# Attention masks copied into PSUM by ScalarE instead of added by a matmul on TensorE

## The chip, the cores and the metric

The kernel runs on one core of one Trainium2 chip, as one launch. The metric is the device time of that launch in microseconds (us). The names of the engines are those of the profile: PE is TensorE, PEld its weight loads, DVE is VectorE, ACT is ScalarE, POOL is GpSimd, and SP issues most of the transfers.

## The reference, cut to what matters

Two transformer-like layers on 4 batches of 512 tokens of width 128. The change touches only the attention of layer 0, causal, with 16 heads of width 8:

```
mask  = where(triu(ones(S, S), k=1), -inf, 0)
score = einsum('bhqd,bhkd->bhqk', Q, K) / sqrt(8)
score = score + mask
score = score - max(score, axis=-1)
score = exp(score);  score = score / sum(score, axis=-1)
out   = einsum('bhqk,bhkd->bhqd', score, V)   # then @ WO
```

After it come a mixture of 8 experts, a gated linear recurrence with a feed-forward part, and a network with ternary weights. They stay as they are.

## The kernel before, in words

Attention works in 16 **groups**: 4 batches times 4 sets of 4 heads (`NW = 16`; `b` is the batch, `g` the set). The scores of a group are computed twice.

**Row scores** serve only for the maximum of each row. They are cut into 10 **units** (the table `UNITS`): unit u is a pair (t, k), 128 queries of tile t against the 128 keys of tile k for 4 heads, so one matmul that fills a whole PSUM bank of 128x512 (`row_scores`, L1802 to L1817, the matmul is L1812). In the four diagonal units, t == k, a second matmul (L1815) multiplies an identity with `mask4`, a 128x512 tile with -1e30 above the diagonal, and adds it to the same bank. Before the change the diagonal units are numbers 1, 4, 5 and 9. DVE reduces each bank to its row maxima (`row_max`, L1172) and gives it back by `row_free`. There are three such banks, taken in turn (`RING`, `ROWB = 3`): the matmul of a unit waits until the unit three before it is reduced. When all ten are reduced, DVE makes the negated maxima (`minus_max`, L1178 to L1182), PE turns them (`turn_max`, L1854) and DVE adds them to the queries (`add_max`, L1186).

**Key scores** are the scores that count, with keys on the partitions, in 12 units n = 0 to 11 (`key_scores`, L1828). ACT takes the exponential of each (`exp_unit`, L761), 128x512 for n = 0 to 3 and 128x384 for the rest; three banks as well, so key unit n waits for exponential n-3. POOL zeroes what lies above the diagonal in their output (L634). PE multiplies with the values (`values`, L1840), ACT copies the result out (`store_sums`, L768), PE turns it (`turn_out`, L1862) and DVE normalises it (L1194, L1195).

Every engine's order is written by hand, and each engine works through its own queue in that order. The loop runs over **turns** w = 0 to 15. Turn w on PE holds, among others: row unit 0 of group w+1, `turn_max(w)`, then key units 8 to 11 of group w-1 and 0 to 3 of group w mixed with row units 1 to 8 of group w+1, then `values` 1 to 3 of group w-1, row unit 9, key units 4 and 5, `turn_out(w-1)`, `values(w, 0)`, key units 6 and 7.

From the second batch on, the rest of the previous batch's layer 0 is woven in: in turns 4, 8 and 12 PE turns the heads (L1868) and ACT copies them (`take_turn`, L779), in turns 5, 9 and 13 PE multiplies with WO (`times_wo`, L1874), DVE adds and takes statistics, ACT normalises (`tail_norm`, L797), in turns 6, 10 and 14 PE turns the normed rows (L1882), ACT copies them (L779 again) and PE computes the router's logits (L1888), and in turns 7 and 11 DVE ranks them. In turns 0, 4 and 8 the queries and keys of the next batch are projected too (L1799, L1800, ACT's L751, DVE's L1162).

In the text "row unit 9" is unit 9 of the row scores, "exp 7" the exponential of key unit 7.

Of the kernel before, what the change touches and what calls it, by code (L numbers as in the profile page):

```python
# [6 lines left out]
ACT = mybir.ActivationFunctionType  # L7
# [13 lines left out]
NG = 4  # L21
# [16 lines left out]
KEYB = 3  # L38
UNITS = [(1, 0), (1, 1), (2, 0), (2, 1), (0, 0), (2, 2), (3, 0), (3, 1), (3, 2), (3, 3)]
PTW = 10 * P  # L40
# [31 lines left out]
def _turns():  # L72

    at = {}
    for w in range(NW):
        before, g = w // NG - 1, w % NG
        at["max", w] = len(at)
        if before >= 0 and g:
            at[("wo", "turn2", "ranks")[g - 1], before] = len(at)
        if before >= 0 and g == 2:  # L80
            at["logits", before] = len(at)
        if w:
            at["out", w - 1] = len(at)
        if before >= 0 and g == 0:
            at["turn", before] = len(at)
    return at
RING = _ring()
TURNS = _turns()
EARLY = {1: 4, 2: 2, 3: 2}

# [25 lines left out]
def build(nc, d):  # L116
    ctx = ExitStack()
    with ctx:
# [220 lines left out]
        pv_done, v_ready = sem("pv_done"), sem("v_ready")  # L339
        mx_done, qm_done = sem("mx_done"), sem("qm_done")  # L340
        varA, rsA, xnA = sem("varA"), sem("rsA"), sem("xnA")
# [382 lines left out]
        def _(act):  # L724
# [28 lines left out]
            def exp_unit(w, n):  # L753
# [4 lines left out]
                if i == 0 and w:  # L758
                    act.wait_ge(pv_done, TB * (w - 1) + js[-1] + 1)
                act.wait_ge(ts_full, NKU * w + n + 1)  # L760
                act.activation(PT[:, i, a:z], bank[ROWB + n % KEYB][:, 0:z - a], ACT.Exp,  # L761
                               scale=float(DK) ** -0.5).then_inc(exp_done, 1)
            def store_sums(w):

# [64 lines left out]
            for w in range(NW):  # L829
# [14 lines left out]
                exp_unit(w, 2)  # L844
                exp_unit(w, 3)
                if w:
                    store_sums(w - 1)
# [8 lines left out]
                if b and g == 1:  # L856
                    tail_numbers(b - 1)
                    tail_norm(b - 1, 0)
                    tail_norm(b - 1, 1)
                exp_unit(w, 6)  # L860
                exp_unit(w, 7)
            exp_unit(NW - 1, 8)
# [902 lines left out]
        def _(pe):  # L1765
# [36 lines left out]
            def row_scores(G, u):  # L1802
# [5 lines left out]
                elif u == 0:  # L1808
                    pe.wait_ge(qs_in[G % 2], 16 * ((G + 1) // 2))
                    pe.wait_ge(kp_in[G % 3], 64 * ((G + 2) // 3))  # L1810
                t, k = UNITS[u]
                mm = pe.matmul(to, QS[:, G % 2, t * P:(t + 1) * P],  # L1812
                               KP[:, G % 3, k, :, :].rearrange("p i n -> p (i n)"), start=True, stop=t != k)
                if t == k:
                    mm = pe.matmul(to, identr[:, :], mask4[:, :, :].rearrange("p i n -> p (i n)"),  # L1815
# [637 lines left out]
```

## Time and profile before

| | us |
|---|---|
| median of 3 runs | 619.7 (617.17 to 621.14) |
| profiled execution, its own time | 618.03 |
| its span in the trace | 616.3 |
| stage the change lies in (turns 0 to 14) | from 26 to 188 |
| PE busy | 576.6 (94%) |
| DVE busy | 413.6 (67%) |
| ACT busy | 329.6 (53%) |
| mask matmuls (L1815) in the trace | 64 |

A row of the timeline gives the start of a run of like instructions, how long it lasts, engine, line, what is written and read, how many, and in brackets how long the engine had been idle and for whom it waited. A matmul of 512 columns lasts some 0.39 us or more from start to end, but the next one starts before it has ended, so matmuls are costed by the distance of their starts and not by their length. The granted clock is 1.00 in the whole stage.

### The profile page before, as it was taken

Reading aid. Unit: us, or ns where it says so; the run is one execution under the profiler, and the core shown is the slowest. Engines: PE = TensorE matmul, PEld = TensorE weight load, DVE = VectorE, ACT = ScalarE, POOL = GpSimd, SP = SyncE. Lnnn points to the kernel's source line nnn. Section 1 sums busy time; section 2 is a strip of 40 time slices with the busy share of each in tenths; the row PEclk is TensorE's granted clock in tenths of the full one; section 3 lists DMA queues with packets and bytes.
Section 4 is the critical chain, followed back from the end, with each engine's and each line's share of the span. In section 5 each row is a group of like instructions: output and inputs, shape, how many; then the busy total and the mean of one; then the engine's idle time right before and its main releaser. Section 6 shows DMA issues by size and latency. Waiting matters only on the chain.

```text
span 616.3 us, 9661 instructions
## 1 busy us (share of the span) xinstructions
PE 576.6 (94%) x3486; PEld 448.1 (73%) x3486; DVE 413.6 (67%) x1012; ACT 329.6 (53%) x582; POOL 177.2 (29%) x196
## 2 busy tenths in 40 slices
PE   7899999999998699999896988999999999998997
PEld 3667676676764479999765776887878877896776
DVE  6788799899884645645679859945688376752420
ACT  5766675675666235766154438525565257533541
POOL 6223132452643735556421240014101130001100
PEclk9999999999999989999998979999999999999999
DMA  4475641442200647751401000000000000000000
GB/s 140 160 278 196 250 135 45 145 127 74 77 27 2 189 136 256 240 203 56 130 1 35 2 0 0 1 1 2 18 1 1 1 1 17 1 2 0 18 0 18
DMA packets 32543, 45.96 MB, mean 75 GB/s; under 512 B 4336, under 2 KB 18160, under 8 KB 32240
## 3 DMA queue, kind: packets, MB, share of 16 engines
q1 hardware_dynamic: 29904, 40.30, 19.9%
q0 software_dynamic: 2304, 4.74, 2.2%
q8 instruction: 28, 0.46, 0.3%
q10 hardware_dynamic: 288, 0.31, 0.1%
q14 instruction: 19, 0.16, 0.1%
HBM read 26.09 MB, written 19.24 MB: 74 GB/s over the span
## 4 chain that ended last, share of the span: by engine, by line
PE 72%; DVE 13%; ACT 7%; issue 5%; POOL 2%; DMA 1%; DVEq 0%; ACTq 0%; POOLq 0%; SPq 0%
PE ps L2204 7%; PE ps L1812 6%; PE ps L1828 5%; PE ps L2226 5%; PE ps L2119 5%; PE ps L1840 5%; PE ps L2227 4%; PE ps L2307 4%; PE ps L2303 4%; PE ps L2304 4%; PE ps L2230 4%; DVE pm L1172 3%; PE ps L2220 2%; PE ps L1815 2%; PE ps L2104 2%
## 5 line engine op out<-in xcount | busy, mean ns | idle before, releaser
L1172 DVE TENSOR_REDUCE pm<-ps 128x4 f32<-128x512 f32 x160 | 102.7, 684 | 16.8 <-PE ps L1812 9.4
L761 ACT ACTIVATE PT<-ps 128x384 f32<-128x384 f32 (+1 forms) x192 | 92.1, 527 | 31.5 <-PE ps L1828 29.0
L634 POOL TENSOR_SCALAR_AFFINE_SELECT PT<-PT 128x512 f32<-128x512 f32 x64 | 40.1, 639 | 115.6 <-ACT PT L761 115.5
L1812 PE MATMUL ps<-KP,QS 128*128 128x512 f32 x160 | 67.6, 437 | 1.8 <-ACT VR L741 0.7
L1828 PE MATMUL ps<-QM,KP 128*128 128x512 f32 (+3 forms) x256 | 65.1, 328 | 0.4 <-ACT PT L761 0.4
L1828 PEld LDWEIGHTS ps<-QM,KP 128*128 128x128 f32 x256 | 42.9, 189 | 18.2 <-ACT PT L761 10.2
L671 POOL DMA_INDIRECT ytok_dram<-zero,rowS x40 | 41.2, 1030 | 34.9 <-DVE zero L1479 24.4
L608 POOL TENSOR_TENSOR rstd<-veps,mhalf 128x4 f32<-128x4 f32 x11 | 12.7, 1154 | 112.6 <-DVE veps L1083 111.2
L1608 DVE TENSOR_TENSOR_SCAN zero<-decay,OG 128x512 f32<-128x512 f32 x32 | 42.0, 1314 | 1.1
L1840 PE MATMUL ps<-PT,V 128*32 128x128 f32 (+3 forms) x512 | 41.5, 439 | 0.0
L973 ACT ACTIVATE hF<-ps,cols 128x512 f32<-128x512 f32 x16 | 11.0, 688 | 55.9 <-PE ps L2307 55.9
L912 ACT ACTIVATE HT<-ps,cols 128x640 f32<-128x640 f32 x32 | 25.5, 796 | 26.0 <-PE ps L2106 25.3
L1812 PEld LDWEIGHTS ps<-KP,QS 128*128 128x128 f32 x160 | 29.9, 188 | 12.7 <-DVE pm L1172 4.8
L1603 DVE SCALAR_TENSOR_TENSOR OG<-ps,cols,vs 128x512 f32<-128x512 f32 x32 | 23.9, 748 | 17.9 <-ACT vs L952 10.3
L2119 PE MATMUL ps<-W,HT 128*128 128x128 f32 x296 | 35.6, 275 | 0.0
L956 ACT ACTIVATE gs<-ps,half_bg 128x512 f32<-128x512 f32 x32 | 22.0, 689 | 24.1 <-PE ps L2230 23.3
L2119 PEld LDWEIGHTS ps<-W,HT 128*128 128x128 f32 x296 | 34.8, 192 | 0.0
L952 ACT ACTIVATE vs<-ps,cols 128x512 f32<-128x512 f32 x32 | 22.0, 687 | 19.4 <-PE ps L2230 19.3
L2204 PEld LDWEIGHTS ps<-lwo,oT 128*128 128x128 f32 x256 | 29.1, 192 | 0.2
L2204 PE MATMUL ps<-lwo,oT 128*128 128x128 f32 x256 | 29.2, 275 | 0.0
L698 POOL TENSOR_TENSOR aT<-OT,aT 128x512 fp32r<-128x512 f32 x12 | 16.9, 1411 | 38.4 <-ACT OT L936 37.0
L680 POOL TENSOR_TENSOR rstd<-veps,mhalf 128x8 f32<-128x8 f32 x3 | 5.3, 1765 | 77.6 <-DVE veps L1569 77.6
(345 smaller groups left out, 1413.5 us busy)
## 6 DMA issues: line engine op xcount, KB each, us to landing
qk_dram<-HL SPq DMA_DIRECT2D x8, 512.0 KB, 3.8
W<-in_eW SPq DMA_DIRECT2D x16, 256.0 KB, 4.8
QS<-qk_dram SPq DMA_DIRECT2D x15, 256.0 KB, 2.7
KP<-qk_dram SPq DMA_DIRECT2D x60, 64.0 KB
xs_dram<-zero SPq DMA_DIRECT2D x4, 645.0 KB, 3.8
XS<-xs_dram SPq DMA_DIRECT2D x8, 322.5 KB, 3.0
qk_dram<-HL SPq DMA_DIRECT2D x8, 256.0 KB, 4.0
ytok_dram<-zero SPq DMA_DIRECT2D x4, 512.0 KB, 4.6
```

What stands on the lines that cost most here:

```text
L634: g.affine_select(out=diag, in_=diag, pattern=[[0, 4], [1, P]], compare_op=ALU.is_ge, fill=0.0, base=0, channel_multiplier=-1).then_inc(se ...
L671: g.indirect_dma_start(out=ytok_dram, out_offset=bass.IndirectOffsetOnAxis(ap=rowS[:, x, j:j + 1], axis=0), in_=YS[:, s, j, :], in_offset= ...
L761: act.activation(PT[:, i, a:z], bank[ROWB + n % KEYB][:, 0:z - a], ACT.Exp, scale=float(DK) ** -0.5).then_inc(exp_done, 1)
L912: act.activation(HT[:, s, f, :].rearrange("p (a n) -> p a n", a=2), ps[:, 2 * (f % 2):2 * (f % 2) + 2, 0:HALF], ACT.Gelu, bias=cols[:, at: ...
L1172: v.tensor_reduce(pm[:, t, k, :], bank[n % ROWB].rearrange("p (i n) -> p i n", n=P), AXX, ALU.max).then_inc(row_free[n % ROWB], 1)
L1608: v.tensor_tensor_scan(st, decay[:, f:f + 1].to_broadcast([P, SEQ]), kv, 0.0, ALU.mult, ALU.add).then_inc(st_done, 1)
L1812: mm = pe.matmul(to, QS[:, G % 2, t * P:(t + 1) * P], KP[:, G % 3, k, :, :].rearrange("p i n -> p (i n)"), start=True, stop=t != k)
L1828: mm = pe.matmul(bank[ROWB + n % KEYB][:, at:at + SEQ - j * P], KP[:, w % 3, j, i, :], QM[:, w % 2, j * P:SEQ], start=True, stop=True)
L1840: mm = pe.matmul(bank[6][32 * i:32 * i + 32, j * P:SEQ], V[:, j * H + g * 4 + i, :], PT[:, i, OFF[j]:OFF[j + 1]], start=(j == 0), stop=(j ...
L2119: mm = pe.matmul(place(j), HT[:, s, f, j * P:(j + 1) * P], W2[:, s, f, :], start=(f == 0 and (j in (PARTS[0][0], PARTS[1][0]) or not follo ...
L2204: mm = pe.matmul(bank[5][:, t * P:(t + 1) * P], src[:, f, t * P:(t + 1) * P], w[:, f, :], start=(f == 0 and t == 0), stop=(f == n - 1), sk ...
L2226: pe.matmul(to, high[n][:, cs], halves_of[:, 0, :], start=True, stop=False)
```

## The change

`UNITS` is put in another order, so that the diagonal units are now numbers 0, 1, 2 and 9. For 50 of the 64 diagonal units, listed in `SEEDS`, ACT copies `mask4` from SBUF into the bank before the scores (`seed`), and the score matmul is issued with start=False, so that it adds to what lies there; it waits for the semaphore `seeded`. The mask matmul of these units is gone. Not listed are all units of groups 0 and 1, and units 1 and 2 of groups 2, 6 and 10; these 14 diagonal units keep the mask matmul. The copy waits, like the score matmul, until the bank's previous unit is reduced. In ACT's queue the copy for unit 9 of group w+1 stands after exp 3 of turn w, those for units 0 and 1 of group w+2 before exp 6 and that for unit 2 between exp 6 and exp 7.

```diff
-UNITS = [(1, 0), (1, 1), (2, 0), (2, 1), (0, 0), (2, 2), (3, 0), (3, 1), (3, 2), (3, 3)]
+UNITS = [(0, 0), (1, 1), (2, 2), (1, 0), (2, 0), (2, 1), (3, 0), (3, 1), (3, 2), (3, 3)]
...
+def _seeds():
+    at = {}
+    for w in range(NW):
+        if 2 <= w + 1 < NW:
+            at[9, w + 1] = len(at)
+        if w + 2 < NW:
+            for u in range(1 if (w + 2) % NG == 2 and w + 2 < NW - 2 else 3):
+                at[u, w + 2] = len(at)
+    return at
...
+            def seed(u, G):
+                if (u, G) in SEEDS:
+                    n = RING[u, G]
+                    act.wait_ge(row_free[n % ROWB], n // ROWB)
+                    act.activation(bank[n % ROWB], mask4[:, :, :].rearrange("p i n -> p (i n)").bitcast(F32),
+                                   ACT.Copy).then_inc(seeded, 1)
...
                 exp_unit(w, 3)
+                seed(9, w + 1)
                 if w:
                     store_sums(w - 1)
...
+                seed(0, w + 2)
+                seed(1, w + 2)
                 exp_unit(w, 6)
+                seed(2, w + 2)
                 exp_unit(w, 7)
...
                 t, k = UNITS[u]
+                sown = (u, G) in SEEDS
+                if sown:
+                    pe.wait_ge(seeded, SEEDS[u, G] + 1)
                 mm = pe.matmul(to, QS[:, G % 2, t * P:(t + 1) * P],
-                               KP[:, G % 3, k, :, :].rearrange("p i n -> p (i n)"), start=True, stop=t != k)
-                if t == k:
+                               KP[:, G % 3, k, :, :].rearrange("p i n -> p (i n)"), start=not sown, stop=t != k or sown,
+                               skip_group_check=sown)
+                if t == k and not sown:
                     mm = pe.matmul(to, identr[:, :], mask4[:, :, :].rearrange("p i n -> p (i n)"),
                                    start=False, stop=True)
```

The first place is ACT's queue in turn 4 and the start of turn 5 (turn 8 reads the same), before the change. HL is the rounded queries or keys of the next batch, OT the turned heads.

```order
63 L751 ACTIVATE HL<-ps 128x512 [waits rs_full,k_planes,q_planes]
64 L751 ACTIVATE HL<-ps 128x512 [waits rs_full]
65 L779 ACTIVATE OT<-ps 128x512 [waits tp_full]
66 L761 ACTIVATE PT<-ps 128x384 [waits ts_full] x2
67 L761 ACTIVATE PT<-ps 128x384 [waits ts_full,pv_done]
```

The same place after the change; L772 is now the exponential, L779 the copy of the mask and L798 `take_turn`.

```order
83 L762 ACTIVATE HL<-ps 128x512 [waits rs_full,k_planes,q_planes]
84 L762 ACTIVATE HL<-ps 128x512 [waits rs_full]
85 L798 ACTIVATE OT<-ps 128x512 [waits tp_full]
86 L779 ACTIVATE ps<-mask 128x512 [waits row_free0]
87 L772 ACTIVATE PT<-ps 128x384 [waits ts_full] x2
88 L772 ACTIVATE PT<-ps 128x384 [waits ts_full,pv_done]
```

The copy for row unit 0 of group 6 has come in behind the copy of the turned heads and ahead of exp 6 and 7.

The second place is PE's queue at the start of turn 5, before the change: row unit 0 of group 6, the turn of the maxima, and what follows up to row unit 3.

```order
226 L1828 MATMUL ps<-QM,KP 128x384 [waits exp_done] x2
227 L1812 MATMUL ps<-KP,QS 128x512 [waits kp_in0,qs_in0,row_free0]
228 L1854 MATMUL ps<-const,MX 128x128 [waits mx_done,tp_free]
232 L1812 MATMUL ps<-KP,QS 128x512 [waits row_free1]
233 L1815 MATMUL ps<-mask,identr 128x512
238 L1812 MATMUL ps<-KP,QS 128x512 [waits row_free2]
239 L1828 MATMUL ps<-QM,KP 128x256 [waits exp_done]
```

The same place after the change (key scores are now L1855, row scores L1838, the mask matmul L1842, the turn of the maxima L1881).

```order
212 L1855 MATMUL ps<-QM,KP 128x384 [waits exp_done] x2
213 L1838 MATMUL ps<-KP,QS 128x512 [waits kp_in0,seeded,qs_in0,row_free0]
214 L1881 MATMUL ps<-const,MX 128x128 [waits mx_done,tp_free]
218 L1838 MATMUL ps<-KP,QS 128x512 [waits row_free1]
219 L1842 MATMUL ps<-mask,identr 128x512
224 L1838 MATMUL ps<-KP,QS 128x512 [waits row_free2]
225 L1842 MATMUL ps<-mask,identr 128x512
226 L1855 MATMUL ps<-QM,KP 128x256 [waits exp_done]
```

Row unit 0 now waits for `seeded` and stands ahead of the turn of the maxima, and row unit 2 of this group has a mask matmul that it did not have.

The third place is PE's queue late in turn 2, before the change, from row unit 9 to the turn of the sums.

```order
129 L1840 MATMUL ps<-PT,V 32x384 [waits sel_done]
133 L1840 MATMUL ps<-PT,V 32x128 [waits sel_done]
135 L1812 MATMUL ps<-KP,QS 128x512 [waits row_free1]
136 L1815 MATMUL ps<-mask,identr 128x512
137 L1828 MATMUL ps<-QM,KP 128x384 [waits exp_done] x2
138 L1862 MATMUL ps<-const,OG 128x128 [waits og_done,tp_free]
140 L1840 MATMUL ps<-PT,V 32x512 [waits og_done,v_ready,sel_done]
```

And after the change (`values` is L1867, the turn of the sums L1889).

```order
124 L1867 MATMUL ps<-PT,V 32x384 [waits sel_done]
128 L1867 MATMUL ps<-PT,V 32x128 [waits sel_done]
130 L1838 MATMUL ps<-KP,QS 128x512 [waits seeded,row_free1]
131 L1855 MATMUL ps<-QM,KP 128x384 [waits exp_done] x2
132 L1889 MATMUL ps<-const,OG 128x128 [waits og_done,tp_free]
134 L1867 MATMUL ps<-PT,V 32x512 [waits og_done,v_ready,sel_done]
```

The mask matmul between row unit 9 and key unit 4 is gone; the turn of the sums still waits for ACT's copy of them (`og_done`).

## Rows read from the trace of the kernel before

**Rows 1.** The page, part 1: busy time, share of the span, instructions

```profile
PE 576.6 (94%) x3486; PEld 448.1 (73%) x3486; DVE 413.6 (67%) x1012; ACT 329.6 (53%) x582; POOL 177.2 (29%) x196
```

**Rows 2.** The page, part 4: the chain that ended last, by engine

```profile
PE 72%; DVE 13%; ACT 7%; issue 5%; POOL 2%; DMA 1%; DVEq 0%; ACTq 0%; POOLq 0%; SPq 0%
```

**Rows 3.** Busy time by window: a plain turn, then turn 7; length, then each engine's

```profile
55.60:65.20 9.60, 9.60 (x72) 6.56 (x71) 7.94 (x16) 6.37 (x14) 2.50 (x4) 1.00 0.48 154
99.10:108.80 9.70, 9.62 (x82) 6.50 (x83) 9.30 (x25) 5.96 (x13) 2.50 (x4) 1.00 0.19 56
```

**Rows 4.** Timeline of DVE in a plain turn, 54 to 65.5 us

```profile
55.68 0.69 DVE L1172 TENSOR_REDUCE pm<-ps 128x4 f32<-128x512 f32 x1 [0.58 <-PE ps L1812]
...
56.88 4.95 DVE L1172 TENSOR_REDUCE pm<-ps 128x4 f32<-128x512 f32 x8
62.72 0.69 DVE L1172 TENSOR_REDUCE pm<-ps 128x4 f32<-128x512 f32 x1 [0.89 <-PE ps L1815]
...
65.29 0.69 DVE L1172 TENSOR_REDUCE pm<-ps 128x4 f32<-128x512 f32 x1 [0.58 <-PE ps L1812]
```

**Rows 5.** Timeline of PE's matmuls in the same turn

```profile
60.53 1.50 PE L1840 MATMUL ps<-PT,V 128*32 128x384 f32 x24
61.96 0.50 PE L1812 MATMUL ps<-KP,QS 128*128 128x512 f32 x1
62.30 0.39 PE L1815 MATMUL ps<-mask,identr 128*128 128x512 f32 x1
62.52 0.52 PE L1828 MATMUL ps<-QM,KP 128*128 128x384 f32 x2
...
64.86 0.40 PE L1812 MATMUL ps<-KP,QS 128*128 128x512 f32 x1
```

**Rows 6.** Timeline of PE's weight loads in the same turn

```profile
60.09 0.19 PEld L1812 LDWEIGHTS ps<-KP,QS 128*128 128x128 f32 x1 [0.30 <-DVE pm L1172]
...
62.81 0.43 PEld L1862 LDWEIGHTS ps<-const,OG 128*128 128x128 f32 x4
```

**Rows 7.** Timeline of ACT in the same turn

```profile
56.36 4.31 ACT L761 ACTIVATE PT<-ps 128x384 f32<-128x384 f32 x8 [0.21 <-PE ps L1828]
62.10 0.60 ACT L768 ACTIVATE OG<-ps 128x512 f32<-128x512 f32 x1 [1.43 <-PE ps L1840]
62.95 0.87 ACT L761 ACTIVATE PT<-ps 128x384 f32<-128x384 f32 x2 [0.26 <-PE ps L1828]
64.88 0.87 ACT L761 ACTIVATE PT<-ps 128x384 f32<-128x384 f32 x2 [1.05 <-PE ps L1828]
```

**Rows 8.** Groups of ACT's instructions by form, 30 to 184 us: busy, mean ns, idle

```profile
L773 ACT ACTIVATE V<-VR 128x512 f32<-128x512 f32 x3 | 1.9, 623 | 0.0
```

**Rows 9.** Timeline of ACT, end of turn 8

```profile
121.04 0.60 ACT L779 ACTIVATE OT<-ps 128x512 f32<-128x512 f32 x1 [0.98 <-PE ps L1868]
121.54 0.87 ACT L761 ACTIVATE PT<-ps 128x384 f32<-128x384 f32 x2
```

**Rows 10.** Timeline of all engines at the start of turn 9

```profile
121.20 0.39 PE L1812 MATMUL ps<-KP,QS 128*128 128x512 f32 x1
...
121.70 0.66 PE L1854 MATMUL ps<-const,MX 128*128 128x128 f32 x4
...
125.37 0.69 DVE L1208 TENSOR_TENSOR X<-ps,X 128x512 f32<-128x512 f32 x1 [0.30 <-PE ps L1874]
```

**Rows 11.** Timeline of ACT, end of turn 5 and turn 6

```profile
86.45 0.88 ACT L797 ACTIVATE xn_rows<-X,nmr,rstd 128x128 f32<-128x128 f32 x2
87.52 0.87 ACT L761 ACTIVATE PT<-ps 128x384 f32<-128x384 f32 x2 [0.20 <-PE ps L1828]
88.78 0.49 ACT L761 ACTIVATE PT<-ps 128x384 f32<-128x384 f32 x1 [0.39 <-PE ps L1828]
...
91.53 0.62 ACT L779 ACTIVATE xn2T<-ps 128x512 f32<-128x512 f32 x1
```

**Rows 12.** Timeline of PE, turn 6

```profile
92.64 0.95 PE L1888 MATMUL ps<-wr,xn2T 128*128 128x8 f32 x8
```

More of the change, by code:

```diff
@@ L86, in _turns @@
     return at
+def _seeds():
[7 more added lines that the diff above has]
+    return at
 RING = _ring()
+SEEDS = _seeds()
 TURNS = _turns()
@@ L339, in build @@
         pv_done, v_ready = sem("pv_done"), sem("v_ready")
-        mx_done, qm_done = sem("mx_done"), sem("qm_done")
+        mx_done, seeded = sem("mx_done"), sem("seeded")
         varA, rsA, xnA = sem("varA"), sem("rsA"), sem("xnA")
```

## The prediction, made before the changed kernel was run

> **What bounds the kernel now.** I read the share of busy time first: PE is busy 94% of the span, ACT and DVE far less [rows 1], and the chain of waits puts 72% on PE [rows 2]. That speaks for taking work off PE. But a busy share adds up matmuls that overlap, and the change lies in one stage, so I went to the windows of that stage. In a plain turn of 9.6 us DVE is busy 7.94, ACT 6.37; in turn 7 DVE is busy 9.30 of 9.70 [rows 3]. So DVE is close behind PE in a plain turn and is the bound in turn 7, as in turn 11, which has the same work.
>
> What a plain turn really waits for shows when the timelines of the engines are laid side by side. DVE reduces row unit 0 at 55.68, then adds the maxima, and from 56.88 reduces units 1 to 8 without a break, 4.95 us for eight, a step of (4.95 - 0.69)/7 = 0.61 [rows 4]. Unit 5 is thus done at 56.88 + 4 x 0.61 + 0.69, near 60.0, and exactly then PE, which sat 0.30 for DVE, loads the weights of row unit 8 [rows 6], the unit that takes the bank of unit 5. Behind it come the values at 60.53 and row unit 9 at 61.96 [rows 5]. ACT, idle 1.43, starts to copy the sums when the values are done, at 62.10, and ends at 62.70 [rows 7]; 0.11 later PE loads the first weights of the turn of the sums, 62.81 [rows 6]. The values of unit 0, key units 6 and 7 and row unit 0 follow, at 64.86 [rows 5], and DVE, idle 0.58 for it, takes that at 65.29 [rows 4]: one turn of 9.61. The loop of the turn is: DVE from unit 0 to unit 5, row unit 8, values, ACT's copy, the turn of the sums, values, key units, row unit 0. **No mask matmul lies on it.** Those of units 1, 4 and 5 lie where PE ends up waiting for DVE; that of unit 9 lies beside ACT's copy of the sums.
>
> **What the change removes.** A mask matmul costs PE the distance to the next start: 62.30 to 62.52, say 0.23 [rows 5]. 50 of them are 11.5 us of PE. In plain turns (1 to 3, 8 and 12) I take the gain as 0.03 each: without the mask PE would be ready for the turn of the sums 0.23 earlier, but ACT's copy ends at 62.70 and the load starts at 62.81 anyway. In turns 7 and 11 DVE is the bound and nothing is gained. Together -0.2.
>
> **What it adds.** 50 copies of 128x512 by ACT. No row shows ACT writing PSUM from SBUF. The nearest are PSUM to SBUF, 0.60 [rows 7], and SBUF to SBUF, 623 ns [rows 8]; I take 0.60 from start to end. When ACT is never idle the next instruction starts 0.50 after such a copy: the turned heads go out at 121.04 and exp 6 starts at 121.54 [rows 9]. So a copy takes 0.50 of ACT's queue. As ends of the range I take 0.50 and 0.75 for the whole length: the step of a queue and half as much again over it. The Trainium skill, "ScalarE: Activation LUTs", section "Step-by-step: what each stage is for", holds that "ScE→PSUM is faster than ScE→SBUF"; no row here shows such a write, and by that rule the lower end, 0.50, would hold and the sum below come out 0.6 lower.
>
> Plain turns: the copy for unit 9 follows exp 3, which ends at 56.36 + 4.31 = 60.67, in an idle stretch of 1.43 [rows 7]. It waits for the reduction of unit 6, near 60.6. Done near 61.3, it is there before row unit 9 at 61.96 [rows 5]. The copies for units 0 and 1 come behind exp 5, which ends at 62.95 + 0.87 = 63.82, in an idle stretch of 1.05 [rows 7]: 2 x 0.50 just fits, and unit 0's is done at 64.4, before row unit 0 at 64.86. The copy for unit 2 pushes exp 7 back by 0.50, and key unit 10 waits for exp 7. There PE loses what the missing mask of unit 1 gave, and DVE, which sets the pace, notices nothing. ACT has 9.6 - 6.4 = 3.2 us free in such a turn [rows 3] and is asked for 2.0. Cost 0, covered by ACT's idle time; should exp 4 to 7 run later than now, it is up to 0.5 per turn (the third rival).
>
> Turns 0 and 1 work on groups 1 and 2, with a mask matmul now on unit 0 (ahead of the turn of the maxima) and on unit 2, where there was none. Each was placed where PE is just in time for DVE: +0.23 each, **+0.5**. The bounds are 0 and 0.9, four masks.
>
> **Turns 5, 9 and 13** hold most of the cost. Now PE issues row unit 0 at 121.20, while ACT copies the turned heads from 121.04, and the turn of the maxima, which waits for that copy to end at 121.64, starts at 121.70 [rows 9, 10]. After the change ACT can begin the mask copy only at 121.54; it ends at 122.14, and row unit 0, which stands ahead of the turn of the maxima in PE's queue, starts near 122.28. The turn of the maxima follows at 122.5 instead of 121.70: +0.8. Between it and the product with WO PE's queue is full, and DVE, idle 0.30 for PE, adds that product at 125.37 [rows 10]; in turns 5 and 9 a mask on unit 2 comes on top, +0.23. In turn 13 a mask less gives 0.23 back, but two more copies ahead of exp 7 make key unit 10 wait some 0.4. So +1.0 three times, **+3.0**; with the ends of the copy's price 2.7 and 3.5.
>
> **Turns 6, 10 and 14.** At the end of the turn before, ACT has no idle time to give: the norms run from 86.45 to 87.33 and exp 6 starts at 87.52 [rows 11]. Three copies there take 1.5 us against idle stretches of 0.20 and 0.39 (before 88.78, where exp 8 starts) and a gap of some 0.1: exp 8 and all behind it come 0.8 later, 0.6 in the other two turns. The copy of the normed rows moves from 91.53 [rows 11] to about 92.4 and ends at 93.1, so that the router's product starts at 93.2 and not at 92.64 [rows 12]; the missing masks between can't help, since it is ACT that is late. +0.5 and twice +0.4, **+1.3**, with bounds 0 and 2.4 (0.8 each). The statistics ahead of it run on DVE and hide nothing.
>
> **Sum:** -0.2 + 0.5 + 3.0 + 1.3 = +4.6 us. What lies behind attention waits for its last group, so I pass this on one to one. The profiled execution took 618.03 us in a span of 616.3; it would take 622.6. It was 1.7 below the median of the runs, 619.7, so for a median I say **624**.
>
> **The rivals.**
> First, PE is the bound, as the shares say [rows 1, 2]. Then 50 x 0.23 = 11.5 us go and the stage gives 608. It decides if DVE could start earlier with what PE brings earlier; against it stand the eight reductions without a break [rows 4] and the 0.30 that PE waits for them [rows 6]. 7%. By the Trainium skill, "TensorE: Matmul & The Clock Gate", section "Back-to-back issue gap", a sustained stream with 512 columns costs 131 ns per matmul, by which this rival would gain only 50 x 0.131 = 6.6 us; the 0.22 between the starts in rows 5 does not agree, and I go by that.
> Second, a part of it: the plain turns gain the mask of unit 9 after all (0.23 x 9 = 2.1), and turns 5, 9, 13 lose half as much as I say: 617 to 619. 8%.
> Third, the copies are hidden everywhere but in a few places: each wait at the start of turns 5, 9 and 13 is swallowed by DVE's own work later in the turn. 618 to 622, that is no change. 20%.
> Fourth, on the slower side beyond my forecast: ACT becomes the bound. The 11 copies for unit 2 push exp 7 back, and in every turn key unit 10 and all behind it come 0.5 late: 11 x 0.5 = 5.5 on top of 4.6, 630. It decides once ACT's late exponentials outlast the 1.43 that it is idle before the copy of the sums [rows 7]. Against it: 0.92 of that are left. 12%.
> The forecast, a loss of 2.5 to 8 us, has the remaining 53%.
>
> A difference of under 1%, 6.2 us, is no change by what a measurement of this kernel can tell. Faster by more is the first rival alone, 7%. Slower by more, over 625.9, is the fourth, 12%, and of the forecast the upper part, about 15%: 27%. The rest is 66%. The range of 8 in 10 takes in the hidden case and the upper bounds of the terms: 617.5 to 629.5.
>
> **What would show it in the changed profile.** L1842 (mask) 14 times, the copy from the mask 50 times at about 0.6. A plain turn of 9.6, with DVE's eight reductions still without a break, and the load for the turn of the sums still 0.11 behind ACT's copy. At the start of turns 5, 9 and 13 row unit 0 waiting for ACT, and the turn of the maxima 0.8 later than ACT's copy of the heads asks for. The router's product 0.4 to 0.5 later in its turn. I am wrong if a plain turn gets shorter than 9.4 or longer than 9.8, or if DVE shows breaks among the eight.

## The result and the profile after

The changed kernel takes 622.2 us (median of 20 runs, 619.6 to 623.5) against 619.7 for the kernel before on the same chip. The ratio is 1.0040 with a 95% interval of 1.0028 to 1.0053: a loss of 2.5 us that can be told from nothing and lies within the 1% that the forecast called no change. The profiled execution has a span of 618.0 us (before 616.3). The page's shares of busy time after the change, beside [rows 1]:

```profile
PE 572.4 (93%) x3436; PEld 436.5 (71%) x3436; DVE 410.3 (66%) x1012; ACT 352.8 (57%) x632; POOL 176.8 (29%) x196
```

PE has lost its 50 matmuls and ACT has gained 50 instructions; where the time went must be read turn by turn. A turn is measured from one reduction `mx<-pm` of DVE (L1178 before, L1201 after) to the next. The last of them, the end of turn 14, in the timeline of DVE before and after:

```profile
186.74 0.26 DVE L1178 TENSOR_REDUCE mx<-pm 128x16 f32<-128x64 f32 x1
```

```profile
189.01 0.26 DVE L1201 TENSOR_REDUCE mx<-pm 128x16 f32<-128x64 f32 x1
```

The attention stage ends 2.27 us later, which is about the loss of the medians. The two profiled spans differ by less, 1.7 us, because what lies behind the stage took 0.6 less in the second. That part isn't equally long from one execution to the next: the kernel before took 429.6 us for it here and 431.4 in a second profile (experiments, third set). So the turns, and not the spans, carry the argument. Lengths of the turns in us, worked out from these rows:

```
turns           0     1   2..4(mean)  5     6     7     8     9    10    11    12    13    14
before       8.19 11.09   9.62   13.39 11.31 10.48  9.42 13.88 11.30 10.42  9.44 12.15 11.31
after        8.41 11.24   9.52   14.47 11.50 10.02  9.15 14.47 11.56  9.95  9.15 13.04 11.96
difference  +0.22 +0.15  -0.10   +1.08 +0.19 -0.46 -0.27 +0.59 +0.26 -0.47 -0.29 +0.89 +0.65
```

**The copy.** The view of line L779 (instructions, their shortest, median and longest duration in ns; then what ended ACT's idle time before them, and who waited for them, in us and times):

```profile
L779 ACT ACTIVATE ps<-mask x50: 577/601/611, 35.4 to 185.1; 128x512 f32<-128x512 f32 x50
...
  DVE pm L1195: 3.7, 11
...
  PE ps L1838: 3.9, 5
```

It takes 0.60 us, as the forecast took it. PE waited for it 3.9 us in 5 places. The Trainium skill's sentence that ScalarE writes PSUM faster than SBUF ("ScalarE: Activation LUTs", section "Step-by-step: what each stage is for") holds here by some 0.02 us, 601 ns against the 623 ns of [rows 8], not by the 0.10 that I gave as its end of the range.

**A plain turn.** DVE in turn 3 (start, busy time, idle before and its releaser), to be laid beside [rows 4]:

```profile
55.98 0.69 DVE L1195 TENSOR_REDUCE pm<-ps 128x4 f32<-128x512 f32 x1 [0.58 <-PE ps L1838]
...
57.18 4.88 DVE L1195 TENSOR_REDUCE pm<-ps 128x4 f32<-128x512 f32 x8
62.71 0.69 DVE L1195 TENSOR_REDUCE pm<-ps 128x4 f32<-128x512 f32 x1 [0.65 <-PE ps L1838]
...
65.50 0.69 DVE L1195 TENSOR_REDUCE pm<-ps 128x4 f32<-128x512 f32 x1 [0.58 <-PE ps L1838]
```

PE's weight loads of the same turn, beside [rows 6]:

```profile
60.32 0.19 PEld L1838 LDWEIGHTS ps<-KP,QS 128*128 128x128 f32 x1 [0.41 <-DVE pm L1195]
...
63.02 0.42 PEld L1889 LDWEIGHTS ps<-const,OG 128*128 128x128 f32 x4 [0.32 <-issue]
```

And ACT's queue, beside [rows 7]:

```profile
60.90 0.60 ACT L779 ACTIVATE ps<-mask 128x512 f32<-128x512 f32 x1 [0.29 <-DVE pm L1195]
62.31 0.60 ACT L787 ACTIVATE OG<-ps 128x512 f32<-128x512 f32 x1 [0.81 <-PE ps L1867]
62.95 0.87 ACT L772 ACTIVATE PT<-ps 128x384 f32<-128x384 f32 x2
63.71 1.12 ACT L779 ACTIVATE ps<-mask 128x512 f32<-128x512 f32 x2
65.09 0.49 ACT L772 ACTIVATE PT<-ps 128x384 f32<-128x384 f32 x1 [0.26 <-PE ps L1855]
```

The loop of the forecast stands, leg by leg. From DVE's unit 0 to the load for row unit 8: 60.09 - 55.68 = 4.41 before, 60.32 - 55.98 = 4.34 after. From there to ACT's copy of the sums 2.01 and 1.99. From that copy to the turn of the sums 0.71 and 0.71. From the turn of the sums to the next unit 0 2.48 and 2.48. Row unit 9, whose mask is gone, reaches DVE 0.31 earlier (62.71 - 57.18 = 5.53 instead of 62.72 - 56.88 = 5.84), and nothing comes of it: the turn of the sums waits for ACT, whose idle time before it fell from 1.43 to 0.81 with room to spare. What was gained, 0.07 of 0.09, lies inside DVE's unbroken eight, 4.95 to 4.88. Asked for in narrower windows, the trace gives the start of each reduction: before the change the next one starts 0.63 after unit 1 and 0.63 after unit 4, which had masks, and 0.60 to 0.61 after the others; after the change all seven steps are 0.59 to 0.61.

**Turn 7.** DVE before and after:

```profile
99.84 0.69 DVE L1186 TENSOR_TENSOR QM<-QS,ps 128x512 fp32r<-128x512 f32 x1
100.55 1.98 DVE L1172 TENSOR_REDUCE pm<-ps 128x4 f32<-128x512 f32 x3
...
102.58 0.21 DVE L1254 TENSOR_TENSOR rank<-ps,const 128x64 f32<-128x64 f32 x1
102.86 2.57 DVE L1172 TENSOR_REDUCE pm<-ps 128x4 f32<-128x512 f32 x4
```

```profile
101.22 0.69 DVE L1209 TENSOR_TENSOR QM<-QS,ps 128x512 fp32r<-128x512 f32 x1
101.82 1.88 DVE L1195 TENSOR_REDUCE pm<-ps 128x4 f32<-128x512 f32 x3
...
103.75 0.21 DVE L1277 TENSOR_TENSOR rank<-ps,const 128x64 f32<-128x64 f32 x1
103.88 2.47 DVE L1195 TENSOR_REDUCE pm<-ps 128x4 f32<-128x512 f32 x4
```

No row shows an idle time, yet from `QM` to the first reduction it is 0.71 before and 0.60 after, from `rank` to the next 0.28 and 0.13, and each group of reductions is 0.10 shorter: 0.46 in all. A reduction lasts 0.69 from start to end, but an unhindered one is followed by the next 0.60 after its start. So DVE can wait up to 0.09 for a unit and no idle time is seen, and the longer record counts as busy: in the whole turn DVE's busy time fell from 9.96 to 9.59 with the same 29 instructions. DVE looked busy for 95% of this turn and had still waited.

**Turn 9.** ACT, PE and DVE at its start, beside [rows 9, 10]:

```profile
121.68 0.60 ACT L798 ACTIVATE OT<-ps 128x512 f32<-128x512 f32 x1 [0.99 <-PE ps L1895]
122.17 0.60 ACT L779 ACTIVATE ps<-mask 128x512 f32<-128x512 f32 x1
```

```profile
122.92 0.47 PE L1838 MATMUL ps<-KP,QS 128*128 128x512 f32 x1 [0.92 <-ACT ps L779]
123.22 0.60 PE L1881 MATMUL ps<-const,MX 128*128 128x128 f32 x4
```

```profile
123.42 0.69 DVE L1195 TENSOR_REDUCE pm<-ps 128x4 f32<-128x512 f32 x1 [1.94 <-PE ps L1838]
124.03 0.68 DVE L1209 TENSOR_TENSOR QM<-QS,ps 128x512 fp32r<-128x512 f32 x1
```

The same place of DVE before the change:

```profile
121.62 0.69 DVE L1172 TENSOR_REDUCE pm<-ps 128x4 f32<-128x512 f32 x1 [0.78 <-PE ps L1812]
122.39 0.69 DVE L1186 TENSOR_TENSOR QM<-QS,ps 128x512 fp32r<-128x512 f32 x1
```

PE waits 0.92 us for the copy, which itself waits behind the copy of the heads, and the turn of the maxima comes 123.22 - 121.68 = 1.54 after ACT starts the heads, where it was 121.70 - 121.04 = 0.66. That is 0.88 later, where 0.8 was forecast. DVE adds the maxima (`QM`) later still, by 1.00: 124.03 - 121.68 = 2.35 against 122.39 - 121.04 = 1.35. Its queue has row unit 0 first, which came only at 123.42, and `QM` starts 0.61 behind that, a step that the forecast left out.

Where a late start ends up is seen from three times in each of these turns, counted from the turn's start, and read in the timelines of DVE in all kernels: the start of `QM`, the start of the addition of the product with WO (L1208 before, L1231 after), and the turn's end. The last three kernels are experiments told below ("unit 2 behind" has unit 2's copy behind exp 7).

```
                     turn 5              turn 9              turn 13
                 QM   WO    end      QM   WO    end      QM   WO    end
before          4.14 7.14 13.39     4.15 7.13 13.88     2.42 5.40 12.15
after           5.15 8.21 14.47     5.15 8.22 14.47     3.43 6.40 13.04
unit 0 first    4.15 7.36 13.62     4.15 7.39 13.87     2.46 5.91 12.87
unit 2 behind   5.15 8.21 14.47     5.15 8.21 14.46     3.43 6.32 12.57
masks left out  4.15 6.91 13.16     4.15 6.88 13.53     2.42 5.18 11.78
```

The forecast named signs by which it could be checked. The 14 masks and 50 copies are there, a plain turn is within 9.4 to 9.8, DVE's eight have no listed break, and the load for the turn of the sums comes 0.11 behind ACT's copy. One sign failed: the router's product starts 5.70 after the start of turn 6, where it was 5.61, so 0.09 later and not 0.4 to 0.5.

### The profile page after: what moved, and what is told of

It reads as the page before. It is cut to its first block, busy times and chain, and to the rows that moved or that the text cites. A ratio compares the mean times of both kernels' runs of the same rounds, so it can differ in the third digit from the quotient of the medians.

```text
span 618.0 us, 9661 instructions
## 1 busy us (share of the span) xinstructions
PE 572.4 (93%) x3436; PEld 436.5 (71%) x3436; DVE 410.3 (66%) x1012; ACT 352.8 (57%) x632; POOL 176.8 (29%) x196
## 4 chain that ended last, share of the span: by engine, by line
PE 60%; DVE 16%; ACT 9%; issue 7%; POOL 5%; DMA 2%; DVEq 0%; ACTq 0%; POOLq 0%; SPq 0%
PE ps L2231 7%; DVE pm L1195 6%; PE ps L2253 5%; PE ps L2146 5%; PE ps L2330 4%; PE ps L2334 4%; PE ps L2331 4%; PE ps L2254 4%; PE ps L2257 4%; PE ps L1867 3%; PE ps L1838 3%; POOL xs_dram L630 3%; PE ps L1855 3%; PE ps L2247 2%; PE ps L2131 1%
## 5 line engine op out<-in xcount | busy, mean ns | idle before, releaser
L1195 DVE TENSOR_REDUCE pm<-ps 128x4 f32<-128x512 f32 x160 | 101.4, 682 | 21.6 <-PE ps L1838 19.5
L772 ACT ACTIVATE PT<-ps 128x384 f32<-128x384 f32 (+1 forms) x192 | 89.9, 529 | 15.1 <-PE ps L1855 13.5
L1838 PE MATMUL ps<-KP,QS 128*128 128x512 f32 x160 | 70.9, 448 | 6.5 <-ACT ps L779 3.9
L1855 PE MATMUL ps<-QM,KP 128*128 128x512 f32 (+3 forms) x256 | 66.8, 330 | 1.3 <-ACT PT L772 1.1
L1855 PEld LDWEIGHTS ps<-QM,KP 128*128 128x128 f32 x256 | 43.5, 189 | 18.1 <-ACT PT L772 11.5
L1838 PEld LDWEIGHTS ps<-KP,QS 128*128 128x128 f32 x160 | 29.8, 187 | 24.5 <-DVE pm L1195 12.1
L1867 PE MATMUL ps<-PT,V 128*32 128x128 f32 (+3 forms) x512 | 41.5, 439 | 0.0
L779 ACT ACTIVATE ps<-mask 128x512 f32<-128x512 f32 x50 | 29.0, 597 | 3.7 <-DVE pm L1195 3.7
L1001 ACT ACTIVATE hB<-ps,cols 128x512 fp32r<-128x512 f32 x16 | 11.0, 690 | 30.3 <-PE ps L2334 30.3
```

What stands on the lines that cost most here:

```text
L779: act.activation(bank[n % ROWB], mask4[:, :, :].rearrange("p i n -> p (i n)").bitcast(F32), ACT.Copy).then_inc(seeded, 1)
L1195: v.tensor_reduce(pm[:, t, k, :], bank[n % ROWB].rearrange("p (i n) -> p i n", n=P), AXX, ALU.max).then_inc(row_free[n % ROWB], 1)
L1838: mm = pe.matmul(to, QS[:, G % 2, t * P:(t + 1) * P], KP[:, G % 3, k, :, :].rearrange("p i n -> p (i n)"), start=not sown, stop=t != k or ...
L1855: mm = pe.matmul(bank[ROWB + n % KEYB][:, at:at + SEQ - j * P], KP[:, w % 3, j, i, :], QM[:, w % 2, j * P:SEQ], start=True, stop=True)
L1867: mm = pe.matmul(bank[6][32 * i:32 * i + 32, j * P:SEQ], V[:, j * H + g * 4 + i, :], PT[:, i, OFF[j]:OFF[j + 1]], start=(j == 0), stop=(j ...
```

## Experiments

The lengths of the turns of all kernels are read as above. The kernel before runs at another median on each chip, so ratios are taken within a set alone: 628.0 us in the first set ("masks left out", "unit 0 first", "order only", "no copies, masks"), 624.2 in the second ("norms by matmul", "copies where free", "copies in four"), 619.0 in the third (the rest). In the first two sets turns 8 and 12 are longer by 0.5 to 2.7 us in most kernels, whatever the edit, with a pause of all engines in them; these two turns are left out of every argument on those sets. Two more values of the table are disturbed and prove nothing: turn 13 of "order only" and of "no copies, masks". There the pause of turn 12 (PE idle 2.16 us in the second) is followed by a stretch of lower granted clock, here in "no copies, masks":

```profile
165.00:167.00 2.00, 2.00 (x10) 1.30 (x7) 0.54 (x4) 0.15 (x1) 0.00 (x0) 0.50 0.00 0
```

The last figure but two is the granted clock, 0.50, the level of 1.2 GHz, where it is 1.00 (2.4 GHz) in all turns of the changed kernel. `QM` comes 3.69 after the start of that turn, where it comes 2.42 with all masks left out. In "masks left out" PE was idle for 2.23 us in turn 12 and the clock stayed at 1.00.

```
turns                  1     3     5     6     7     9    10    13    14
before              11.09  9.60 13.39 11.31 10.48 13.88 11.30 12.15 11.31
after               11.24  9.52 14.47 11.50 10.02 14.47 11.56 13.04 11.96
masks left out      10.75  9.52 13.16 10.97 10.02 13.53 11.18 11.78 11.17
unit 0 first        11.24  9.54 13.62 11.50 10.03 13.87 11.61 12.87 11.74
norms by matmul     11.26  9.53 14.47 11.00 10.03 14.64 11.04 13.33 11.40
order only          11.49 10.03 13.62 11.02 10.46 13.87 11.25 13.47*11.23
no copies, masks    11.24  9.52 13.62 10.95 10.02 13.87 11.02 13.00*11.02
copies where free   11.07  9.53 13.39 11.00 10.04 13.88 11.04 12.15 11.03
copies in four      11.47  9.99 14.74 12.32 10.36 14.74 12.37 14.23 12.54
masks behind WO     10.97  9.52 13.21 11.01 10.02 13.22 10.98 11.50 10.97
unit 2 after exp 7  11.24  9.52 14.47 11.51 10.02 14.46 11.56 12.57 12.03
```

\* with the lower clock; not used.

**Masks left out of the kernel before.** It leaves out all 64 masks, with no copies in their place.

```diff
-                               KP[...], start=True, stop=t != k)
-                if t == k:
+                               KP[...], start=True, stop=True)
+                if False:
```

> The kernel before, with all 64 mask matmuls left out of the row scores (what is computed changes only in that row maxima are taken over the keys above the diagonal too). Theory: few of them lie on the path. Plain turns 2 to 4 shorter by 0.1 each, 8 and 12 by 0.3, 7 and 11 by 0.5, 5, 9, 13 by 0.2, 6, 10, 14 by at most 0.45: together -3.8 us, ratio 0.994. Rival, PE is the bound of the stage: 64 x 0.23 = -14.7 us, ratio 0.976.

Measured: 624.6 us, ratio 0.9961 (0.9931 to 0.9992). All 64 masks together are worth 0.4% of the kernel's time, at most 0.7%, and not the 2.3% that 64 x 0.23 = 14.7 us gives. The first rival, PE as the bound, falls. A plain turn is 9.52, as in the changed kernel.

**Row unit 0's copy ahead of the heads'.** The changed kernel with the copy moved by one place in ACT's queue in turns 4, 8 and 12.

```diff
                 if b and g == 0:
+                    seed(0, w + 2)
                     take_turn("turn", b - 1, OT[:, :])
...
-                seed(0, w + 2)
+                if not (b and g == 0):
+                    seed(0, w + 2)
```

> The changed kernel, with the copy for row unit 0 put ahead of ScalarE's copy of the turned heads in turns 4, 8 and 12. Theory: the 0.8 to 0.9 us by which the turn of the maxima comes late in turns 5, 9 and 13 goes, because the copy falls into the 0.99 that ScalarE is idle there: -2.5 us against the changed kernel, so 1.000 against the kernel before. Rival, those turns lose their time to the two mask matmuls on units 1 and 2 and to VectorE: no difference to the changed kernel, 1.004.

Measured: 628.6 us, ratio 1.0001 (0.9969 to 1.0033). Turn 5 falls from 14.47 to 13.62 and turn 9 from 14.47 to 13.87; turn 13 only from 13.04 to 12.87. PE and ACT in turn 5:

```profile
76.73 0.39 PE L1840 MATMUL ps<-KP,QS 128*128 128x512 f32 x1
77.22 0.66 PE L1883 MATMUL ps<-const,MX 128*128 128x128 f32 x4
```

```profile
75.48 0.60 ACT L779 ACTIVATE ps<-mask 128x512 f32<-128x512 f32 x1
...
76.57 0.60 ACT L798 ACTIVATE OT<-ps 128x512 f32<-128x512 f32 x1 [0.49 <-PE ps L1897]
```

The row scores no longer wait, and the turn of the maxima starts 0.65 after ACT starts the heads, as before the change. So the late copy costs 0.85 in turn 5, and 0.23 (13.62 against 13.39) is the new mask on unit 2. In turn 9 the fall is 0.60 only because a small instruction of DVE, `nm`, takes 0.40 here and 0.17 in the changed kernel (see the last section); the product with WO comes 0.83 earlier. In turn 13 `QM` comes 0.97 earlier, but the product only 0.49, and the turn ends only 0.17 earlier. The first half is lost on key unit 10, behind ACT's late exp 7:

```profile
167.53 0.45 PE L1857 MATMUL ps<-QM,KP 128*128 128x256 f32 x2 [0.46 <-ACT PT L772]
```

The second, 0.32, goes at the end of the turn, where ACT starts to copy the sums only after 1.94 idle (0.87 in the changed kernel). Why it starts so late was not followed up.

**Turns 6, 10 and 14 by matmul.** The changed kernel without the copies for units 0 to 2 among the norms.

```diff
-        if w + 2 < NW:
+        if w + 2 < NW and (w < NG or w % NG != 1):
```

> The changed kernel without the copies for units 0, 1 and 2 that ScalarE makes at the end of turns 5, 9 and 13, among the norms (groups 7, 11, 15 take these masks by matmul again). Theory: exp 8 and the norms behind it come in time again, and masks 4 and 5 stay off the stretch to the router's product: turns 6, 10, 14 go from 11.50, 11.56, 11.96 to what the order alone had, 11.0 to 11.25, -1.5 us, so 1.0015 of the kernel before. Rival, it was the waits of TensorE for the copies of row units and not ScalarE's late queue: the mask matmuls bring the same delay, 1.004.

Measured: 625.3 us, ratio 1.0030 (1.0008 to 1.0051). The three turns come down to 11.00, 11.04 and 11.40. ACT's copy of the normed rows in turn 6, first in the changed kernel and then here:

```profile
93.23 0.63 ACT L798 ACTIVATE xn2T<-ps 128x512 f32<-128x512 f32 x1
```

```profile
92.71 0.62 ACT L798 ACTIVATE xn2T<-ps 128x512 f32<-128x512 f32 x1
```

The two turns start 0.03 apart, so the copy comes 0.49 earlier. In exchange for the same masks by matmul, the copies cost 0.50, 0.52 and 0.56 in these turns, as ACT's work. Turns 9 and 13 are 0.17 and 0.29 longer here than in the changed kernel, for which no row was looked for, and the ratio over the whole run, at which 1.0015 was expected, is less sharp than the turns.

**Order only.** The new order of the units, every mask by matmul.

```diff
-        if 2 <= w + 1 < NW:
+        if False:
...
-        if w + 2 < NW:
+        if False:
```

> The changed kernel's order of units (diagonal ones 0, 1, 2, 9) with all masks added by matmuls again and no copies. Theory: the mask of unit 0 stands ahead of the turn of the maxima, which lies on the loop of the turn, and unit 2's makes VectorE wait: +0.2 to 0.35 in most of 15 turns, +3 to +5 us, ratio 1.005 to 1.008. Rival, the place of a mask does not matter: 1.000.

Measured: 630.3 us, ratio 1.0042 (1.0014 to 1.0069). A plain turn becomes 10.03, half a microsecond over the changed kernel's 9.52 and 0.4 over the old order's. A mask on row unit 0 stands ahead of the turn of the maxima, which is on the loop; DVE then waits 0.81 for unit 0 where it waited 0.58, and 0.18 once within the eight:

```profile
57.15 0.69 DVE L1195 TENSOR_REDUCE pm<-ps 128x4 f32<-128x512 f32 x1 [0.81 <-PE ps L1842]
...
59.22 4.28 DVE L1195 TENSOR_REDUCE pm<-ps 128x4 f32<-128x512 f32 x7 [0.18 <-PE ps L1842]
```

The old order had put the masks where they cost less; most of what the copies save in a plain turn, 0.41 of 0.51, is a price that the new order first sets. In turn 6 it is the other way round: with every mask in place the new order alone brings 11.31 down to 11.02.

**Neither copies nor their masks.** The changed kernel with 50 masks left out and no copies; 14 mask matmuls stay.

```diff
-                if (u, G) in SEEDS:
+                if False:
...
-                if sown:
-                    pe.wait_ge(seeded, SEEDS[u, G] + 1)
...
-                               KP[...], start=not sown, stop=t != k or sown, skip_group_check=sown)
+                               KP[...], start=True, stop=t != k or sown)
```

> The changed kernel without its 50 copies, and without the waits for them, the 50 masks being left out (the 14 mask matmuls stay). Its distance to the changed kernel is what copies and waits cost, its distance to the order alone what 50 mask matmuls cost. Theory: copies cost some 2.5 at the starts of turns 5, 9, 13 and 2.5 in turns 6, 10, 14 and 0 in plain turns: 5 to 5.5 us, so this one at 0.9955 of the kernel before. Rival, the copies cost only the late starts of turns 5, 9, 13: 0.9995. Rival, ScalarE is the bound in plain turns: a plain turn well under the 9.52 of the changed kernel, ratio 0.990 or less.

Measured: 627.5 us, ratio 0.9992 (0.9961 to 1.0023). Turns 3 and 7 are 9.52 and 10.02, the changed kernel's own: there the copies cost nothing at all. Turns 6 and 10 are 10.95 and 11.02, so their +0.19 and +0.26 are two things: -0.36 and -0.28 for the new order with the masks gone, +0.55 and +0.54 for the copies. In turn 6 the order alone makes 0.29 of the 0.36; in turn 10 it makes 0.05 of the 0.28. The ratio, 0.9992 and not the expected 0.9955, is too coarse to decide on this: in this kernel's trace the pauses and the lower clock make turns 8, 12 and 13 some 4 us longer than undisturbed ones, and the kernel before has no trace on this chip to set beside it. The pause that sets turns 8 and 12 of these sets apart looks so on PE, here in turn 8:

```profile
117.64 0.63 PE L1886 MATMUL ps<-const,OG 128*128 128x128 f32 x4 [0.79 <-issue]
```

Its cause isn't known; it doesn't appear in the third set.

**Copies where ACT is free.** The old order for groups 0, 1, 2, 6, 10 and 14 and no copies for units 0 to 2 of groups 2, 6, 7, 10, 11, 14 and 15; 35 copies and 29 mask matmuls remain. The last line of the diff stands in both places where `UNITS` is read.

```diff
+LATE = [(1, 0), (1, 1), (2, 0), (2, 1), (0, 0), (2, 2), (3, 0), (3, 1), (3, 2), (3, 3)]
+LATE_GROUPS = (0, 1, 2, 6, 10, 14)
...
-            for u in range(1 if (w + 2) % NG == 2 and w + 2 < NW - 2 else 3):
+            for u in range(0 if w + 2 in (2, 6, 7, 10, 11, 14, 15) else 3):
...
-                t, k = UNITS[u]
+                t, k = (LATE if G in LATE_GROUPS else UNITS)[u]
```

> Copies only where ScalarE has idle time for them: unit 9 of groups 2 to 15, and units 0, 1, 2 of groups 3, 4, 5, 8, 9, 12, 13 (35 copies, 29 mask matmuls). Groups 0, 1, 2, 6, 10, 14 keep the units in the order of the kernel before, groups 7, 11, 15 have the new order with matmuls on units 0, 1, 2. Theory, turn by turn against the kernel before: 1 to 4 -0.1 each, 6, 10, 14 -0.3, -0.1, -0.1, 7 and 11 -0.46 each, 8 and 12 -0.28 each, 0, 5, 9, 13 nothing: -2.4 us, ratio 0.996. Rival, the gains of turns 7 and 8 came from work that the losses before them had put off: no gain there, ratio 0.999.

Measured: 622.7 us, ratio 0.9983 (0.9964 to 1.0003). The gain over the whole run can't be told from nothing. Turns 5, 9 and 13 are back at 13.39, 13.88 and 12.15, those of before, while turns 3, 6, 7 and 10 keep their gain. (In turn 9 the agreement is a coincidence: the product with WO comes 0.21 later than before and `nm` is 0.21 shorter.) The losses are bound to those places and not to the copies as such.

**Each copy as four of 128 columns.** Raises ACT's cost of a copy, with PE's work unchanged.

```diff
-                    act.activation(bank[n % ROWB], mask4[:, :, :].rearrange("p i n -> p (i n)").bitcast(F32),
-                                   ACT.Copy).then_inc(seeded, 1)
+                    for i in range(4):
+                        ins = act.activation(bank[n % ROWB][:, i * P:(i + 1) * P], mask4[:, i, :].bitcast(F32), ACT.Copy)
+                    ins.then_inc(seeded, 1)
```

> The changed kernel with each of the 50 copies made as four of 128 columns, which takes ScalarE some 0.8 to 1.2 in place of 0.5 each. It asks how much room plain turns still have. ScalarE is busy 6.4 of 9.5 and has 2.0 of copies now; with 3.2 to 4.8 it has less than nothing left. Theory: plain turns 2 to 4 grow from 9.52 by 0.2 to 1.0 each, turns 5, 9, 13 by 0.3 to 0.7, 6, 10, 14 by 0.5 to 1.5, in all +5 to +12 over the changed kernel. Rival, ScalarE never matters outside turns 5, 9, 13: plain turns stay at 9.52, in all +1 to +2.

Measured: 634.3 us, ratio 1.0171 (1.0142 to 1.0200). Four take 0.88 from start to end, and a plain turn grows to 9.99. ACT, PE and DVE in turn 3:

```profile
56.86 0.88 ACT L780 ACTIVATE ps<-mask 128x128 f32<-128x128 f32 x4
```

```profile
58.19 0.44 PE L1856 MATMUL ps<-QM,KP 128*128 128x256 f32 x2 [0.47 <-ACT PT L772]
```

```profile
58.96 4.28 DVE L1196 TENSOR_REDUCE pm<-ps 128x4 f32<-128x512 f32 x7 [0.39 <-PE ps L1839]
```

This is the fourth rival in the flesh: exp 7 is late, key unit 10 waits 0.47 for it, and DVE's eight break. That is with copies 0.28 longer each. At 0.60 a copy fits; lengths between were not tried.

**Before and changed kernel once more, on the chip of the third set.**

> The kernel before, unchanged, for its trace on the chip of the experiments. In the experiments turn 8 lasts 9.8 to 9.9 us where the changed kernel's trace has 9.15, and turn 12 9.6 to 11.3. If that belongs to the chip or its state and not to the edits, turn 8 is here about 0.7 over its 9.42 too, and turns 2 to 7 are as they were to 0.05.

> The changed kernel, unchanged, beside the one before: turns 2 to 7 9.52, 9.52, 9.52, 14.47, 11.50, 10.02; turn 8 9.85 if the extra time belongs to the chip, 9.15 if it belongs to the edits of the experiments.

Both as they were, without an edit. Measured: 620.4 and 622.2 us. All turns repeat to 0.04 us, turns 8 and 12 with 9.42 and 9.42 before and 9.15 and 9.14 changed; so the longer ones of the first two sets belong to those sets and not to the edits.

**Masks behind the product with WO.** As "copies where free", but the diagonal units of the late groups are numbers 4, 5, 6 and 9.

```diff
-LATE = [(1, 0), (1, 1), (2, 0), (2, 1), (0, 0), (2, 2), (3, 0), (3, 1), (3, 2), (3, 3)]
+LATE = [(1, 0), (2, 0), (2, 1), (3, 0), (0, 0), (1, 1), (2, 2), (3, 1), (3, 2), (3, 3)]
```

> As the kernel with copies only where ScalarE is free, but groups 0, 1, 2, 6, 10, 14 have their diagonal units at 4, 5, 6 and 9, so that no mask matmul stands between the turn of the maxima and the product with WO. Theory: the 0.23 of that mask leaves turns 5, 9 and 13 (13.16, 13.65, 11.9), turns 0 and 1 gain 0 to 0.3: -0.9 us against that kernel, ratio 0.997 of the kernel before. Rival, VectorE sets the time of turns 5, 9, 13: no difference.

Measured: 614.8 us against 619.0, ratio 0.9927 (0.9902 to 0.9953), faster than both kernels. PE in turn 5:

```profile
79.08 1.05 PE L1903 MATMUL ps<-wo,OT 128*128 128x128 f32 x8
79.89 0.47 PE L1840 MATMUL ps<-KP,QS 128*128 128x512 f32 x1
80.20 0.39 PE L1844 MATMUL ps<-mask,identr 128*128 128x512 f32 x1
```

The masks stand behind the product that DVE waits for. Turn 5 gains 0.18 for the mask of unit 1. Turns 9 and 13 gain 0.66 and 0.65, which is more than the same mask: 0.46 and 0.47 of it is `nm`, told below. In the table this kernel is, from turn 3 on, at most 0.05 longer in a turn than the one with all masks left out: there its masks cost next to nothing. Whether such an order would do as well with no copy at all was not tried.

**Unit 2's copy behind exp 7.** The changed kernel with one line moved.

```diff
-                seed(2, w + 2)
                 exp_unit(w, 7)
+                seed(2, w + 2)
```

> The changed kernel with the copy for row unit 2 behind exp 7 instead of ahead of it. Theory: key unit 10 no longer waits for exp 7, which shows in turn 13 alone (-0.2 to -0.4 of 13.04); exp 8 is as late as before, so turns 6, 10, 14 stay, and plain turns stay at 9.52. Rival, exp 7 is what makes turns 6, 10 and 14 late: they get shorter by 0.5 each.

Measured: 620.1 us, one run. Turn 13 is 12.57 instead of 13.04, the others unchanged, 6, 10 and 14 too (14 is 12.03 against 11.96), so exp 7 isn't what makes them late. Turn 13 seems to bear out the charge of 0.4 for a late exp 7, but its rows say otherwise. DVE's small `nm`, first in the second run of the changed kernel and then here:

```profile
174.22 0.58 DVE L1244 TENSOR_SCALAR nm<-mv 128x4 f32<-128x4 f32 x1
```

```profile
174.11 0.17 DVE L1244 TENSOR_SCALAR nm<-mv 128x4 f32<-128x4 f32 x1
```

`nm` starts 0.11 earlier here, and the turns begin 0.04 apart (164.01 and 163.97), so the move is worth 0.07; the other 0.41 is `nm` itself. Key unit 10 had waited only 0.19:

```profile
168.06 0.45 PE L1855 MATMUL ps<-QM,KP 128*128 128x256 f32 x2 [0.19 <-ACT PT L772]
```

## Why the forecast held, and where not

The forecast was a loss of 4.6 us by a mechanism with four terms; measured are 2.5, or 2.24 as the sum of the turns. The waits that it named are there, at the turns that it named. But two terms that were taken as nothing were not nothing, and inside the two large terms some sizes were wrong and made up for each other. The measured loss lies at the lower edge of the 2.5 to 8 that was called the forecast.

- **Turns 0 and 1, +0.5:** +0.22 and +0.15. Right but for 0.13. With the masks of these groups behind the product with WO, turn 1 takes 10.97 and turn 0 is as before (8.18).
- **Turns 5, 9 and 13, +3.0:** +2.56, and without `nm`, which took 0.49 less in turn 9 and 0.10 less in turn 13, +1.08, +1.08 and +0.99. The +1.0 is right each time, but not by the right parts. In all three turns `QM` comes 1.00 to 1.01 late and not 0.8, because DVE must reduce the late row unit 0 first. In turns 5 and 9 the mask on unit 2 then adds only 0.06 and 0.09 to the way from `QM` to the product; when the start is in time ("unit 0 first") it adds 0.21 and 0.26. In turn 13 the way from `QM` to the product is as long as before, 2.97 and 2.98: the missing mask gives back what the late exp 7 takes. For that 0.4 was charged; PE waited 0.19, and moving the copy gained 0.07. In that turn the two waits overlap: with the first taken away ("unit 0 first") the second grows from 0.19 to 0.46.
- **Turns 6, 10 and 14, +1.3:** +1.10, but as the sum of +0.5 for the copies in each and something less. The step "the missing masks between can't help, since it is ACT that is late" failed: -0.36 in turn 6, shown with the copies gone, though 0.29 of that comes with the order alone. The copies' own price is 0.50 to 0.56 each, 1.6 and not 1.3.
- **Plain turns and 8 and 12, -0.03 each:** turns 2, 3, 4, 8 and 12 have -0.11, -0.08, -0.11, -0.27, -0.29, a sum of -0.86 (turn 1 is counted above; the forecast's list left out turn 4). The legs of the loop are as they were read; the term was mis-sized, because masks on units 1 and 4 made DVE 0.03 late each within the "unbroken" eight. In turn 12 it was more, as in turn 7: from `QM` to the first reduction 0.71 before and 0.61 after, the eight 5.03 and 4.87. So "no mask matmul lies on it" was not quite so.
- **Turns 7 and 11, nothing:** -0.46 and -0.47. This is the step that failed by size: "DVE is the bound and nothing is gained". [rows 3] has DVE busy 9.30 of 9.70, and the forecast read that as an engine that can't go faster. It was waiting for units with masks, and when the masks went, the waits went.

The last two errors are of one kind and make up 1.6 of the difference of 2.4 between forecast and trace; 0.1 comes from turns 0 and 1, 0.2 from turns 6, 10 and 14 and 0.4 from 5, 9 and 13, where `nm` alone took 0.59 off.

Of the rivals the first fell with "masks left out". The third, that DVE swallows the waits of turns 5, 9 and 13, has those turns against it, though the measured 622.2 lies only just above its 618 to 622. The fourth is real only for a dearer copy, as "copies in four" shows. The second is right in part, a gain in plain turns, but by units 1 and 4 and not by that of unit 9.

## What to carry to other kernels

In this kernel, moving work from the busiest engine to one with idle time cost nothing where the receiving queue had idle time at that very position, and cost 0.5 to 1.0 us where the queue already had something urgent: read idle time at the position in the queue, not per turn. Where the masks stood mattered as well as which engine made them: 50 copies and 14 mask matmuls lost 2.5 us, 35 copies and 29 mask matmuls at other places gained 4.2, of which some 0.9 is `nm`. So try also to put such work behind what the next engine waits for. And an engine that a page shows busy 96% of a window can still be waiting: compare the steps between its instructions with the same step elsewhere before calling it the bound.

## What was not expected of the hardware

- A TENSOR_SCALAR on DVE of 128x4, `nm<-mv`, took 0.17 us in some executions of a place and up to 0.66 in others, and moved the end of the turn with it. In turn 9, before the change and after it, with what POOL does beside it:

```profile
129.18 0.65 POOL L634 TENSOR_SCALAR_AFFINE_SELECT PT<-PT 128x512 f32<-128x512 f32 x1
129.20 0.66 DVE L1221 TENSOR_SCALAR nm<-mv 128x4 f32<-128x4 f32 x1
```

```profile
130.32 0.64 POOL L645 TENSOR_SCALAR_AFFINE_SELECT PT<-PT 128x512 f32<-128x512 f32 x1
130.92 0.17 DVE L1244 TENSOR_SCALAR nm<-mv 128x4 f32<-128x4 f32 x1
```

  It repeats within a kernel (0.65 and 0.17 in their second profiles). In all 39 places in the 13 traces it goes by POOL: where an instruction of POOL runs when `nm` starts and goes on for 0.15 us or more, `nm` ends 0.02 to 0.05 after it; where it goes on for 0.10 or less, or none runs, `nm` takes 0.17. That holds for POOL's issue of a DMA too (L630 from 173.80 for 0.96, `nm` from 174.23 for 0.56, in turn 13 of the changed kernel). So what the change does to `nm` is a shift of the two engines against each other, and chance as far as the forecast goes. No run moved POOL's work to test it. Of the 4.2 us that "masks behind WO" gains, some 0.9 is this.
- A copy of 128x512 from SBUF to PSUM on ACT takes 0.60 us, like one from PSUM to SBUF, and four of 128 columns take 0.88.
- Whether the scores were added to the copied mask, or replaced it, can't be told from these runs. The row maxima only shift the exponents, so up to rounding the output is the same without any mask on the row scores, as in "masks left out"; a mask that was overwritten would leave no sign in it. The times hold either way.
